# A graph attention kernel: TensorE's semaphore updates gathered into one per quad

## What is computed

```python
for l in range(L):                      # L = 2, H = 8 heads of 16
    xn = _layernorm(x, ln1_g[l], ln1_b[l])
    ...
    q, k, v = ...                       # xp @ Wq[l], Wk[l], Wv[l]
    att = jnp.einsum('ehd,ehd->eh', q[dst], k[src]) / scale     # per edge
    att = jnp.nan_to_num(jnp.clip(att, -50.0, 50.0), ...)
    ex = jnp.exp(att - m[dst])
    s = jax.ops.segment_sum(ex, dst, num_segments=n)
    msg = (v[src] * alpha[:, :, None]).reshape(-1, D)
    aggr = jax.ops.segment_sum(msg, dst, num_segments=n)
    x = x + (aggr @ Wo[l] + bo[l])
    h = jax.nn.gelu(_layernorm(x, ln2_g[l], ln2_b[l]) @ W1[l] + b1[l], approximate=False)
    x = x + (h @ W2[l] + b2[l])
```

## Time and profile before

| | us |
|---|---|
| median of 3 runs | 3509.81 |
| lowest and highest | 3503.63, 3520.41 |
| span of the profiled execution | 3472.7 |
| TensorE busy in it | 2377.0 (68%) |
| VectorE busy | 1981.1 (57%) |
| GpSimd busy | 1820.8 (52%) |
| ScalarE busy | 1704.5 (49%) |

### The profile page before, as it was taken

One profiled execution on the slowest core, in us unless ns is written; L12 is line 12 of the kernel. 1 busy time (PEld: TensorE's weight loads), 2 busy tenths in 40 slices (PEclk: granted clock), 3 DMA queues, 4 the chain that ended last, 5 costly groups with the idle time before them and its releaser, 6 DMA issues.

```text
span 3472.7 us, 60241 instructions
## 1 busy us (share of the span) xinstructions
PE 2377.0 (68%) x13853; PEld 2027.0 (58%) x13854; DVE 1981.1 (57%) x7060; ACT 1704.5 (49%) x4472; POOL 1820.8 (52%) x1968
## 2 busy tenths in 40 slices
PE   6998774567667676777667746666666666666667
PEld 6988333556556565656556635556565565565556
DVE  7887782455555555555556625555555455554555
ACT  6765653345445444545445434354444445454444
POOL 5642655655555555555555245556555555555552
PEclk9999885778878878878888867788778778787788
DMA  7865232222322222222223122222222222222221
GB/s 211 242 207 172 88 106 85 85 77 84 89 86 84 84 79 85 79 86 82 82 83 88 45 72 83 82 81 84 81 77 78 81 79 81 77 81 81 78 84 37
DMA packets 180176, 323.48 MB, mean 93 GB/s; under 512 B 38740, under 2 KB 93991, under 8 KB 179892
## 3 DMA queue, kind: packets, MB, share of 16 engines
q0 software_dynamic: 80208, 216.22, 21.7%
q1 hardware_dynamic: 98948, 103.44, 9.7%
q10 hardware_dynamic: 736, 0.93, 0.1%
HBM read 288.09 MB, written 20.71 MB: 89 GB/s over the span
## 4 chain that ended last, share of the span: by engine, by line
another core or an unknown queue 15%; PE 13%; issue 10%; DVE 8%; DVEq 3%; ACT 3%; ACTq 0%; DMA 0%; SPq 0%
PE bank L2080 5%; DVE aggregate L2120 3%; PE bank L2071 2%; PE bank L1729 2%; PE bank L1723 1%; DVE arena L2128 1%; ACT arena L2013 1%; PE bank L2056 1%; PE bank L1720 1%; DVE arena L2148 1%; DVEq L2109 1%; DVE arena L2162 1%; DVEq L2120 1%; PE bank L1718 1%
## 5 line engine op out<-in xcount | busy, mean ns | idle before, releaser
L1992 POOL DMA_INDIRECT arena<-kv_rows,idx_stage x1612 | 1540.8, 956 | 1344.6 <-DVE arena L2128 798.4
L2080 PE MATMUL bank<-arena 128*128 128x136 f32 x3328 | 698.7, 359 | 654.1 <-DVE aggregate L2120 551.8
L2120 DVE TENSOR_TENSOR aggregate<-bank,aggregate 128x136 f32 x1664 | 493.9, 297 | 1017.6 <-remote 851.3
L2080 PEld LDWEIGHTS bank<-arena 128*128 128x128 f32 x3328 | 589.1, 249 | 746.1 <-DVE aggregate L2120 419.9
L2071 PE MATMUL bank<-queries,arena 128*128 x3328 | 547.5, 317 | 82.0 <-DVE arena L2148 53.6
L2071 PEld LDWEIGHTS bank<-queries,arena 128*128 128x128 f32 x3328 | 509.9, 233 | 91.3 <-issue 90.8
L2013 ACT ACTIVATE arena<-iota_n,at_negdst 128x128 f32<-128x128 f32 x1664 | 527.7, 395 | 3.8 <-DMA kv_rows<-arena 2.0
L1777 ACT ACTIVATE arena<-bank 128x256 f32<-128x256 f32 (+1 forms) x225 | 85.0, 379 | 731.8 <-remote 454.8
L2056 PE MATMUL bank<-ident,arena 128*128 128x128 f32 x1664 | 325.7, 329 | 106.1 <-issue 63.0
L2148 DVE TENSOR_TENSOR arena<-bank,arena 128x512 f32<-128x512 f32 x416 | 284.6, 684 | 152.8 <-remote 68.2
L2037 ACT ACTIVATE arena<-arena 128x32 f32<-128x32 f32 x416 | 92.8, 223 | 556.0 <-DVE arena L2177 336.3
(11 more groups left out here) (322 smaller groups left out, 2796.3 us busy)
## 6 DMA issues: line engine op xcount, KB each, us to landing
arena<-in_edge_attr_dram SPq DMA_DIRECT2D x244, 256.0 KB
arena<-kv_rows,idx_stage POOLq DMA_INDIRECT x1612
kv_rows<-arena SPq DMA_DIRECT2D x12, 512.0 KB, 3.8
kv_rows<-arena SPq DMA_DIRECT2D x24, 256.0 KB, 2.2
arena<-in_x_dram SPq DMA_DIRECT2D x12, 256.0 KB, 4.0
x_rows<-arena SPq DMA_DIRECT2D x12, 256.0 KB, 2.9
x_stream<-arena SPq DMA_DIRECT2D x12, 256.0 KB, 2.3
queries<-arena SPq DMA_DIRECT2D x12, 256.0 KB, 2.7
```

Source lines behind the costliest of these rows:

```text
L1992: pool.indirect_dma_start(kv[:, n, :], None, kv_dram[l], bass.IndirectOffsetOnAxis(idx_stage[:, half % 2, n:n + 1], 0)).then_inc(Z.kv_in[s ...
L2080: pe.matmul(sums_of(j), sel[:, r % SEL_SLOTS, j, :], msg[:, r % 2, j, :], start=True, stop=True).then_inc(Z.sum, 1)
L2120: dve.tensor_tensor(a, sums_of(j), a, ALU.add).then_inc(Z.added, 1)
```

## The change

Three semaphores (`Z.selt`, `Z.qe`, `Z.sum`) become one, `Z.quad`. TensorE updates it once per body, at the last of the four sums; in body 0, which has no sums, at the last query product; and before the first body four times for the first four quads' transposes and once for the first two quads' query products. `passed_by(l, i)` is the count after body i; what a waiter used to look up in three semaphores it now looks up as "TensorE has passed body i". Waits on transposes of quad k become waits on body k-4, on query products on body k-2, and on sums on body k+1. `copy_t` loses its second wait, and of the four `join` calls only the first waits for TensorE. `up` makes two updates, one per gap, in place of four. No matmul is added, left out or moved.

```diff
@@ update_steps
-                "pe": (("aggt", "o", "zt") + each("up", UPS) + ("down",), ("xt",) + each("qkv", t)),
+                "pe": (("aggt", "o", "zt", "up1", "up3", "down"), ("xt",) + each("qkv", t)),
@@ pe_update
             def up(u, gap):
                 for k in range(gap * UPS // 2, (gap + 1) * UPS // 2):
-                    pe.matmul(...).then_inc(u.sem("pe"), 1)
+                    last = pe.matmul(...)
+                last.then_inc(u.sem("pe"), 1)
@@
+        AHEAD = 5
+        PASSES = AHEAD + AT_QUADS + 1
+        def passed_by(l, i):
+            return l * PASSES + AHEAD + 1 + i
+        def spread_by(l, k):
+            return l * PASSES + AHEAD if isinstance(k, int) and k < 2 else passed_by(l, k - 2)
+        def turned_by(l, k):
+            return l * PASSES + 1 + k if isinstance(k, int) and k < 4 else passed_by(l, k - 4)
+        def summed_by(l, k):
+            return passed_by(l, k + 1)
@@ act_attention
             def copy_t(k, r):
-                act.wait_ge(Z.selt, k0 + k + 1)
-                if not (isinstance(k, int) and k < SELT_SLOTS):
-                    act.wait_ge(Z.qe, k0 + k - SELT_SLOTS + 1)
+                act.wait_ge(Z.quad, turned_by(l, k))
@@ pe_attention
-                m.then_inc(Z.selt, 1)
+                return last
...
-                m.then_inc(Z.qe, 1)
+                return last
...
-                    pe.matmul(sums_of(j), sel[:, r % SEL_SLOTS, j, :], msg[:, r % 2, j, :],
-                              start=True, stop=True).then_inc(Z.sum, 1)
+                    last = pe.matmul(sums_of(j), sel[:, r % SEL_SLOTS, j, :], msg[:, r % 2, j, :], start=True, stop=True)
+                last.then_inc(Z.quad, 1)
@@ dve_attention
             def add(k, j, tile):
-                dve.wait_ge(Z.sum, (k0 + k) * QUAD + j // 2 * 2 + 2)
+                if j == 0:
+                    dve.wait_ge(Z.quad, summed_by(l, k))
...
-                    dve.wait_ge(Z.qe, k0 + k + 1)
+                    dve.wait_ge(Z.quad, spread_by(l, k))
```

More of the change, by code:

```diff
@@ L1728, in up @@
                 for k in range(gap * UPS // 2, (gap + 1) * UPS // 2):
-                    pe.matmul(u.chunk(k), w_up[l][:, k * P:(k + 1) * P], u["t"], start=True, stop=True).then_inc(u.sem("pe"), 1)
+                    last = pe.matmul(u.chunk(k), w_up[l][:, k * P:(k + 1) * P], u["t"], start=True, stop=True)
+                last.then_inc(u.sem("pe"), 1)
             def down(u):
@@ L1913, in weighted @@
                     if u.again:
-                        dve.wait_ge(*u_before(u).done("pe", "up0"))
+                        dve.wait_ge(*u_before(u).done("pe", "up1"))
                         dve.sem_inc(Z.turn, 1)
@@ L1941, in __init__ @@
                 self.dist = sem("dist_ready")
-                self.selt = sem("selt_ready")
                 self.selt_sb = sem("selt_copied")
-                self.qe = sem("q_spread")
+                self.quad = sem("quad_passed_by_pe")
                 self.prod = sem("prod_ready")
@@ L1949, in __init__ @@
                 self.msg = sem("msg_ready")
-                self.sum = sem("summed")
                 self.added = sem("added")
@@ L2016, in select @@
                 if not (isinstance(k, int) and k < SEL_SLOTS):
-                    act.wait_ge(Z.sum, (k0 + k - SEL_SLOTS + 1) * QUAD)
+                    act.wait_ge(Z.quad, summed_by(l, k - SEL_SLOTS))
                 act.activation(sel[:, r % SEL_SLOTS, :, :], dist, ACT.Relu, scale=-1.0, bias=1.0).then_inc(Z.sel, 1)
             def copy_t(k, r):
-                act.wait_ge(Z.selt, k0 + k + 1)
-                if not (isinstance(k, int) and k < SELT_SLOTS):
-                    act.wait_ge(Z.qe, k0 + k - SELT_SLOTS + 1)
+                act.wait_ge(Z.quad, turned_by(l, k))
                 act.activation(sel_t[:, r % SELT_SLOTS, :, :], bank[:, ATT_BANK[0][r % 2], :].rearrange("p (j e) -> p j e", j=QUAD),
@@ L2035, in body @@
                     if not (first and r < 2):
-                        act.wait_ge(Z.sum, (k0 + k - 1) * QUAD)
+                        act.wait_ge(Z.quad, summed_by(l, k - 2))
                     act.activation(msg[:, r % 2, :, D:MW], att[:, r % 2, 2, :].rearrange("p (j h) -> p j h", j=QUAD),
@@ L2070, in spread @@
                 for j in range(QUAD):
-                    m = pe.matmul(bank[:, ATT_BANK[1][r % 2], j * D:(j + 1) * D], sel_t[:, r % SELT_SLOTS, j, :],
-                                  q_all[:, bass.ds(tiles[j], 1), :].rearrange("p t d -> p (t d)"), start=True, stop=True)
-                m.then_inc(Z.qe, 1)
+                    last = pe.matmul(bank[:, ATT_BANK[1][r % 2], j * D:(j + 1) * D], sel_t[:, r % SELT_SLOTS, j, :],
+                                     q_all[:, bass.ds(tiles[j], 1), :].rearrange("p t d -> p (t d)"), start=True, stop=True)
+                return last
             def sums(k, r):
@@ L2090, in body @@
                     if not (last and r + 2 >= QUADS):
-                        spread(k + 2, r + 2, ahead[r % GROUP * QUAD:])
+                        spreading = spread(k + 2, r + 2, ahead[r % GROUP * QUAD:])
+                        if first and r == 0:
+                            spreading.then_inc(Z.quad, 1)
                     update(i, r, 0)
@@ L2096, in pe_attention @@
             for n in range(4):
-                transposes(n, n)
+                transposes(n, n).then_inc(Z.quad, 1)
             begin = load_tiles(0, 2 * QUAD)
             for n in range(2):
-                spread(n, n, begin[n * QUAD:])
+                begun = spread(n, n, begin[n * QUAD:])
+            begun.then_inc(Z.quad, 1)
             run_bodies(pe, body)
@@ L2125, in weigh @@
                 if not (isinstance(k, int) and k < 2):
-                    dve.wait_ge(Z.sum, (k0 + k - 1) * QUAD)
+                    dve.wait_ge(Z.quad, summed_by(l, k - 2))
                 s = r * QUAD % KV_SLOTS
```

2 lines of the change are left out of this document (1 added, 1 removed).

## The result

The changed kernel takes 3526.93 us (median of 20 runs, 3508.19 to 3538.88), the kernel before 3511.57 us (20 runs, 3501.95 to 3526.85). The ratio is 1.0035, with a 95% interval of 1.0023 to 1.0046: a loss of 15 us, real but within the half per cent that I had called no change. The forecast was 3230 us.

What follows compares the result with a forecast made beforehand. It took TensorE's late semaphore updates, 521 us of unexplained chain time, as what bounds the kernel: 3472.7 - 380 + 100 = 3193 us, plus 37.1 us to the median gives 3230 us, range 2960 to 3540 us.

Steps and rivals of the forecast that it cites:

- each update in the line costs a wait of its own: TensorE's semaphore updates queue while GpSimd issues gathers, each delayed in turn, so fewer updates mean less late news; -380 us.
- 0.73 x 521 us = -380 us: Gain term: share of TensorE's updates that goes, times the chain's unexplained time; bounds from nothing to all 521 us.
- The 521 us: 15% of the 3472.7 us span, chain time with no known cause, placed in VectorE's and ScalarE's waits on TensorE.
- The right rival: Gathers hold the head of TensorE's updates, whatever their number; no change, 3500 to 3530 us; chance 0.14.
- The later first add, +100 us: VectorE's first add waits for all four sums, 0.81 us in 247 quads; half of 200 us entered, ends 0 and +200.
- half of 247 x 0.81 us: Quads whose first add did not already wait long, times its new wait: 200 us if all shows, +100 entered.
- ScalarE's copy, 0: Copy of transposes in the node update waits about 2 us later, but the exponential waits for VectorE's logits anyway; 0 entered.
- The 37.1 us: Distance of the median of the runs above the profiled span of the kernel before, carried over: 3193 to 3230 us.
- The price of an increment: About 26 ns per TensorE update, one after another: 2168 fewer give 57 us, 3453 us; chance no more than 0.03.

Runs made afterwards that it cites:

- Plain transfers: Kernel before with each indirect gather replaced by a same-size transfer of fixed rows: 2387.44 us against 3468.9 us on chip 8, ratio 0.6881.
- the first pair's: Changed kernel plus one update per quad: second sum updates its own semaphore, for which VectorE's first add waits; 0.9973 to 0.9976 without the waits, 0.9894 with, of before.

## Why the prediction was wrong

**The step that failed is "each update in the line costs a wait of its own".** I had read two things from the earlier trace rows: the news was late and not the work, and it came in an order. The first holds in every run of a kernel with gathers on chips of that kind. The second I took for a queue with a price per entry, and from it I took 0.73 x 521 us = -380 us. The runs with 84% more and 31% fewer updates move the time by +0.14% and -0.11%, neither told from zero, and the changed kernel has 164 remote waits for 169. The term is nothing, as its lower bound had said. I gave that case 0.14 and took a proportion for which no row had varied the number. The 521 us were a misreading besides: they are the unexplained part of a chain that covers only the time from 1634 us on, not all that the whole span holds of it. A larger figure would have put the forecast further off.

What should have told me was in the earlier trace rows: two semaphores are fulfilled within 0.02 us of each other, though sums, transposes and a query product stood between or behind them. A line that charges per entry would have set them apart; a gate that opens lets them through together. The 10 and 13 us between the three releases at the layer's start I put down to their order, and the third product of after waits 20.71 us with one update in play.

**The right rival** was the second: the head is held by the gathers, not by the number. It said 3500 to 3530 us, and 3526.93 came. That the number fits so well is in part luck: it had neither a gain nor a loss in it, and the runs show one of each, which nearly cancel. Plain transfers on chip 8 show that the gathers are what it hangs on; the 1.76 and 1.88 us between the last gather's end and the release fit it. The 5.34 and 5.00 us at the layer's start, and the 39 releases in the middle of a stretch, do not fit "the end of a run of gathers" as the only gate.

**The later first add, +100 us**, is right in kind and place. Its size without the waits is the distance between the changed kernel and the first pair's, 1.0051 against 0.9976, 0.9973 and 0.9974, that is 0.75% to 0.78% or 20 to 21 us, across different chips. With the waits it is 1.0035 against 0.9894, 1.4% or some 50 us, measured on two chips and so an estimate, with 0.9853 to 0.9934 as the interval of its larger part. I had entered half of 247 x 0.81 us because GpSimd's 5.0 us per quad would cover the rest. On the chips without the waits GpSimd streams without a pause and covers more than I allowed; on the others +100 was about twice that estimate. The waits that the change adds there are 180.1 - 92.2 = 88 us in the profile, not all of them on the path.

**ScalarE's copy, 0**: no gain came from undoing it on a chip without the waits, and the wait it saved went to the logits, as the prediction argued. With the waits it is open; there the kernel with the first pair's news gains although its copy waits 469.2 us for late news.

**What is left of the gain.** The merged updates of transposes and query products, without the late first add, give 0.25% on chips without the waits and 1.06% on chip 8. The number of updates doesn't explain it. With the waits, leaving 932 out gave 0.9989 (0.9969 to 1.0008), at most 0.31%, and in proportion at most 0.58% for the 1752 that the first pair's kernel leaves out. Without them, 2496 more cost at most 0.04%, 0.23% and 0.14% by their intervals, which in proportion is 0.16% or less for 1752. What remains is that the waits themselves fall together: the copy waits for one semaphore and not two, and the products and copies are let go at the end of a body. Which of these gives it wasn't tried. The prediction has no term for it.

**The 37.1 us** are the distance between one short execution and the median one, not a time outside the span, which is 2.1 us. Carrying them over did no harm: 3509.81 - 380 + 100 = 3230 us is the same forecast.

**The price of an increment.** The rows of this case show TensorE's news late by 5 us and more, and the Trainium skill, "VectorE: DVE Perf Modes", section "The TRN2 errata", asks to space dense increments on completion. On chips 9, 5, 11 and 3 the number of increments, from 31% fewer to 84% more, made no difference, so no run here agrees with it as a rule for time; of deadlock, which is what that page of the Trainium skill speaks of, they show nothing. The Trainium skill, "TensorE: Matmul & The Clock Gate", section "The cost: per-tile semaphore tail", puts an increment at about 26 ns, one after another, for small matmuls packed side by side. For the 2496 added ones that would be 65 us if all lay on the path, an estimate from that figure of the Trainium skill; the four runs give -2.8, 0, -1 and +5.9 us.

## What to carry to other kernels

When a wait has no releaser in the trace, vary its suspected cause before giving it a proportion: whether two waits of different age end at the same instant tells a gate from a queue. Merging semaphore updates was worth 0.25% here on chips without late news and 1.06% on one with it, and it delays whoever used the early one; merge only those whose waiter would not have started sooner. Here the best kernel keeps the first pair's news and merges the rest: 0.9974 of the kernel before without the waits and 0.9894 with them, where the changed kernel has 1.0051 and 1.0035.

## What the runs showed of the hardware

On two of six chips that these experiments used, and where the result was measured, TensorE's news arrives late while GpSimd issues indirect gathers back to back: 5 us on average before VectorE's adds, and over 20 us at a layer's start. Most releases come after the end of a stretch of gathers, with a median of 1.84 us in the trace of before, but at the first layer's start it was 5.00 and 5.34 us, and one came at 568.55 us with gathers before and behind it, so the end of a stretch isn't all that opens the gate. On the other four the same kernel streams gathers for whole layers with the news on time, and is 23% faster: 2696 to 2699 us against 3469 to 3525. With plain transfers the difference is gone, 2387.44 us on chip 8 against 2385.94 to 2391.47 on the four.

What makes a chip of the one kind or the other stays open, as does the way in which gathers hold the news. That shorter stretches of gathers would free it on a chip with the waits wasn't tried, since the one pause that was tried, waiting for the landing, met chips without them.
